# Moving two matmul stages of a recurrent layer across the sweep boundary, and the weight features ahead of the first normalisation

## What is computed

```python
xn = (x - mean) / sqrt(var + 1e-5)                       # over 1024 features
ab, AB = xis, exp(xis)
def rfs(z): return AB/32 * exp(z @ (ab*proj).T - 0.5*sum(z*z)*ab*ab)
s = rfs(xn) @ rfs(input_weights).T                       # feats @ weights.T
h = silu((xn @ w1.T)*w1s) * ((xn @ w2.T)*w2s)            # 1024 -> 4096
h = gelu((h @ h1.T)*h1s)                                 # 4096 -> 4096
h = gelu((h @ h2.T)*h2s)                                 # 4096 -> 4096
y = x + s * silu((h @ w3.T)*w3s)                         # 4096 -> 1024
```

## Time and profile before

| | us |
|---|---|
| median of three timed runs | 3020.2 |
| lowest and highest | 2763.45, 3207.62 |
| the profiled execution, device time | 2765.2 |
| its span, first to last instruction, slowest core (core 3) | 2763.6 |
| spans of the eight cores | 2758.9 to 2763.6 |
| TensorE busy in the span | 2629.6 (95%) |
| ScalarE, VectorE busy | 360.9, 251.2 |
| DMA queue of the weights, share of 16 engines' span | 86.4% |

### The profile page before, as it was taken

How to read it: one execution, slowest core, us unless ns; L and a number is a source line. 1 busy time by engine, 2 the same in 40 slices (tenths; PEclk the granted TensorE clock), 3 DMA queues, 4 the chain that set the end, 5 groups by cost and what they waited for, 6 DMA issues and landing times.

```text
span 2763.6 us, 28227 instructions; the slowest of 8 cores (2758.9 to 2763.6 us)
## 1 busy us (share of the span) xinstructions
PE 2629.6 (95%) x12054; PEld 1183.1 (43%) x12054; DVE 251.2 (9%) x382; ACT 360.9 (13%) x498; POOL 205.4 (7%) x391
## 2 busy tenths in 40 slices
PE   1699999999999999999999999999999999999995
PEld 0244444444444444444444444444444444444442
DVE  2213100000013300000013210000002200000001
ACT  0122101010121211010112200101012111010100
POOL 0100000000100000000010000000000000000000
PEclk9899999999999999999999999999999999999997
DMA  5818988888887899999997899999999899999993
GB/s 86 129 30 143 154 153 152 153 152 152 149 166 128 138 154 153 152 153 152 152 151 142 135 160 153 153 152 152 153 142 155 136 155 156 153 153 152 153 152 75
DMA packets 67115, 396.25 MB, mean 143 GB/s; under 512 B 7328, under 2 KB 11696, under 8 KB 21936
## 3 DMA queue, kind: packets, MB, share of 16 engines
q0 software_dynamic: 57408, 377.51, 86.4%
q1 hardware_dynamic: 9584, 16.92, 2.4%
HBM read 763.51 MB, written 8.39 MB: 279 GB/s over the span
## 4 chain that ended last, share of the span: by engine, by line
PE 94%; DMA 3%; DVE 1%; ACT 1%; issue 0%; POOL 0%; DVEq 0%; SPq 0%; ACTq 0%; POOLq 0%
PE pb L480 64%; PE pb L507 8%; PE pb L403 8%; PE pb L380 8%; PE pb L443 2%; PE pb L357 2%; DMA xt_sweep<-xT 1%; PE pb L329 1%; DMA wring<-w2p 1%; DMA xt_r<-xT 1%; ACT t L520 0%; PE pb L163 0%; PE pb L165 0%; DVE h_sb L417 0%; POOL xt_sweep L223 0%
## 5 line engine op out<-in xcount | busy, mean ns | idle before, releaser
L480 PE MATMUL pb<-h_sb,wring 128*128 128x512 bf16 x4096 | 884.7, 379 | 0.0
L480 PE MATMUL pb<-g_sb,wring 128*128 128x512 bf16 x4096 | 884.7, 379 | 0.0
L480 PEld LDWEIGHTS pb<-h_sb,wring 128*128 128x128 bf16 x4096 | 400.5, 98 | 484.8 <-issue 2.3
L480 PEld LDWEIGHTS pb<-g_sb,wring 128*128 128x128 bf16 x4096 | 400.8, 98 | 483.3
L507 PE MATMUL pb<-h_sb,wring 128*128 128x512 bf16 x1024 | 231.1, 389 | 18.8 <-ACT t L520 18.8
L380 PE MATMUL pb<-xn_fm,wring 128*128 128x512 bf16 x1024 | 233.2, 381 | 2.7 <-DMA wring<-w1p 2.7
L403 PE MATMUL pb<-xn_fm,wring 128*128 128x512 bf16 x1024 | 231.5, 379 | 0.6 <-DMA wring<-w2p 0.6
L527 DVE TENSOR_TENSOR s_sb<-t,s_sb 128x512 f32<-128x512 bf16 x32 | 22.1, 692 | 1970.5 <-ACT t L520 1967.7
L491 ACT ACTIVATE h_sb<-pb,h2s_c 128x512 bf16<-128x512 f32 x128 | 88.0, 687 | 796.4 <-PE pb L480 787.2
L491 ACT ACTIVATE g_sb<-pb,h1s_c 128x512 bf16<-128x512 f32 x128 | 88.0, 687 | 692.6 <-PE pb L480 683.1
L507 PEld LDWEIGHTS pb<-h_sb,wring 128*128 128x128 bf16 x1024 | 102.1, 100 | 147.2 <-issue 32.6
(11 more groups left out here) (72 smaller groups left out, 401.1 us busy)
## 6 DMA issues: line engine op xcount, KB each, us to landing
wring<-h1p POOLq DMA_DIRECT2D x128, 1024.0 KB, 10.2
wring<-h2p POOLq DMA_DIRECT2D x128, 1024.0 KB, 10.1
wring<-w1p POOLq DMA_DIRECT2D x32, 1024.0 KB, 14.3
wring<-w2p POOLq DMA_DIRECT2D x32, 1024.0 KB, 10.6
wring<-w3p POOLq DMA_DIRECT2D x32, 1024.0 KB, 10.0
xt_r<-xT SPq DMA_DIRECT2D x32, 256.0 KB, 5.0
y<-s_sb SPq DMA_DIRECT2D x32, 256.0 KB, 5.1
xt_sweep<-xT POOLq DMA_DIRECT2D x32, 128.0 KB, 11.7
```

The costliest lines, as they stand in the source:

```text
L480: ii = t.matmul(p[quad[og]][:, :], wring[:, slot, k8, og * 128:(og + 1) * 128], src_sb[:, kk * 8 + k8, :], start=(kk == 0 and k8 == 0), st ...
```

## The change

- `emit_wphase` and its VectorE squares move from between strip 1 and smm of sweep 0 to the very start: the squares ahead of the first `ln2_squares`, the matmuls between `ln2_stats(0)` and `ln2_bcast_affine(0, 0)`. They use `h_sb` 0 to 15.
- dot0 and smm become functions. In sweep 0 they run where they did. For sweep `s_ + 1`, dot0 is now written in sweep `s_` between h2 and w3, and smm behind the whole end of sweep `s_`, behind its adds, loads and stores. The next sweep then starts with strip 0 of FFN1.
- `emit_xts_loads(s_ + 1)` moves from the start of the sweep to behind the weight loads of strip 2, `ln2_squares` from behind strip 2 to behind strip 3, `ln2_stats` from behind strip 4 to behind strip 5.
- The block of set-up code (first DMAs, memsets, small vectors, `ring_load`) moves up in the file, in the same order; nothing in it is changed.

```diff
+        need(v, cast_sem["iwT"], 16)
+        sq_done = 0
+        for j in range(8):
+            sq_done = V(lambda j=j: v.tensor_mul(
+                h_sb[:, 2 * j:2 * j + 2, :].rearrange("p a b -> p (a b)"),
+                iw_c[j], iw_c[j]))
 
         ln2_squares(0, 0)
...
         ln2_stats(0)
+        emit_wphase()
         xn_ready_sweep = ln2_bcast_affine(0, 0)
 
-        for s_ in range(NS):
-            tok0 = s_ * TS
-
-            if s_ + 1 < NS:
-                emit_xts_loads(s_ + 1)
-
+        def emit_dot0(xn_rdy):
             need(t, cast_sem["projT"], 16)
...
-            feats_done = cS.n
+            return cS.n
+
+        def emit_smm(feats_done):
+            need(t, cS, feats_done)
+            need(t, cS, wstate["wt_done"])
+            for oc in range(8):
+                bk = oc % 4
+                guard_bank(bk)
+                for rc in range(8):
+                    ii = t.matmul(p[bk][:, :], Wt_sb[:, rc, oc * 128:(oc + 1) * 128],
+                                  feats[:, rc, :], start=(rc == 0), stop=(rc == 7))
+                stop = cT.inc(ii)
+                need(v, cT, stop)
+                need(v, d_y[oc], y_val.get(oc, 0))
+                ev = V(lambda oc=oc, bk=bk: v.tensor_copy(s_sb[:, oc, :], p[bk][:, :]))
+                bank_guard[bk] = (cV, ev)
+            return cT.n
...
-            ffn1_strip(0)
-            ffn1_strip(1)
-
             if s_ == 0:
...
+                feats_done = emit_dot0(xn_ready_sweep)
+                ffn1_strip(0)
+                ffn1_strip(1)
+                smm_last = emit_smm(feats_done)
+                first_strip = 2
+            else:
+                smm_last = smm_next
+                first_strip = 0
+
+            for ss in range(first_strip, 8):
                 ffn1_strip(ss)
                 if ss == 2 and s_ + 1 < NS:
+                    emit_xts_loads(s_ + 1)
+                if ss == 3 and s_ + 1 < NS:
                     ln2_squares(s_ + 1, smm_last)
-                if ss == 4 and s_ + 1 < NS:
+                if ss == 5 and s_ + 1 < NS:
                     ln2_stats(s_ + 1)
...
+            if s_ + 1 < NS:
+                feats_next = emit_dot0(xn_ready_sweep)
 
             sg_done = [0] * 8
...
                 y_val[dc] = d_y[dc].n
 
+            if s_ + 1 < NS:
+                smm_next = emit_smm(feats_next)
+
```

More of the change, by code:

```diff
@@ L145, in S @@
             return cS.inc(instr_fn())
[L147 to L206, removed]
@@ L287, in ring_load, with ln2_squares, ln2_stats @@
             return slot, d_wr[slot], d_wr[slot].n
+        xsq = feats
+        ln_state = {}
+        def ln2_squares(s_, smm_last):
+            need(v, cT, smm_last)
+            need(v, d_xts, d_xts.n)
+            for j in range(8):
+                V(lambda j=j: v.tensor_mul(xsq[:, j, :], xt_sweep[:, j, :],
+                                           xt_sweep[:, j, :]))
+            ln_state["sq"] = cV.n
+        def ln2_stats(s_):
+            need(t, cV, ln_state["sq"])
+            guard_bank(6)
+            guard_bank(7)
+            for j in range(8):
+                t.matmul(p[6][0:1, :], ones_b[:, 0:1], xt_sweep[:, j, :],
+                         start=(j == 0), stop=(j == 7))
+                ii = t.matmul(p[7][0:1, :], ones_b[:, 0:1], xsq[:, j, :],
+                              start=(j == 0), stop=(j == 7))
+            st = cT.inc(ii)
+            need(v, cT, st)
+            V(lambda: v.tensor_copy(rows[0:1, 0, :], p[6][0:1, :]))
+            ev = V(lambda: v.tensor_copy(rows[0:1, 1, :], p[7][0:1, :]))
+            bank_guard[6] = (cV, ev)
+            bank_guard[7] = (cV, ev)
+            V(lambda: v.tensor_scalar_mul(rows[0:1, 0, :], rows[0:1, 0, :], 1.0 / D))
+            V(lambda: v.tensor_scalar_mul(rows[0:1, 1, :], rows[0:1, 1, :], 1.0 / D))
+            V(lambda: v.tensor_mul(rows[0:1, 2, :], rows[0:1, 0, :], rows[0:1, 0, :]))
+            sv = V(lambda: v.tensor_sub(rows[0:1, 1, :], rows[0:1, 1, :], rows[0:1, 2, :]))
+            need(sc, cV, sv)
+            S(lambda: sc.activation(rows[0:1, 2, :], rows[0:1, 1, :], AF.Ln,
+                                    bias=c_eps[0:1, 0:1]))
+            rs = S(lambda: sc.activation(rows[0:1, 2, :], rows[0:1, 2, :], AF.Exp,
+                                         scale=c_nhalf[0:1, 0:1]))
+            need(v, cS, rs)
+            V(lambda: v.tensor_mul(rows[0:1, 3, :], rows[0:1, 0, :], rows[0:1, 2, :]))
+            rd = V(lambda: v.scalar_tensor_tensor(rows[0:1, 1, :], rows[0:1, 2, :],
+                                                  512.0 * EPS, rows[0:1, 2, :],
+                                                  op0=ALU.mult, op1=ALU.mult))
+            ln_state["rows"] = rd
@@ new lines, in ln2_bcast_affine @@
+        def ln2_bcast_affine(s_, ffn1_last):
+            need(t, cV, ln_state["rows"])
+            guard_bank(4)
+            guard_bank(5)
+            bc1 = cT.inc(t.matmul(p[4][:, :], ones_row[0:1, :], rows[0:1, 2, :],
+                                  start=True, stop=True))
+            bc2 = cT.inc(t.matmul(p[5][:, :], ones_row[0:1, :], rows[0:1, 3, :],
+                                  start=True, stop=True))
+            need(v, cT, bc2)
+            need(v, cT, ffn1_last)
+            for j in range(8):
+                V(lambda j=j: v.tensor_mul(ln_tmp[:, :], xt_sweep[:, j, :], p[4][:, :]))
+                V(lambda j=j: v.tensor_sub(xn_fm[:, j, :], ln_tmp[:, :], p[5][:, :]))
+            xr = V(lambda: v.tensor_copy(xn_fm[0:1, 8, :], rows[0:1, 1, :]))
+            bank_guard[4] = (cV, xr)
+            bank_guard[5] = (cV, xr)
+            xts_state["guard"] = xr
+            return xr
@@ L301, in emit_wphase @@
         def emit_wphase():
-            need(t, cV, wstate["sq_done"])
+            need(t, cV, sq_done)
             need(t, cast_sem["iwT"], 16)
@@ L306, in emit_wphase @@
             for j in range(8):
-                sqv = h_sb[:, 16 + 2 * j:18 + 2 * j, :].rearrange("p a b -> p (a b)")
+                sqv = h_sb[:, 2 * j:2 * j + 2, :].rearrange("p a b -> p (a b)")
                 t.matmul(p[4][0:1, :], ones_nh[:, 0:1], sqv[:, 0:512],
@@ L340, in build_nc @@
         ln2_stats(0)
+        emit_wphase()
         xn_ready_sweep = ln2_bcast_affine(0, 0)
-        for s_ in range(NS):
-            tok0 = s_ * TS
-            if s_ + 1 < NS:
-                emit_xts_loads(s_ + 1)
+        def emit_dot0(xn_rdy):
             need(t, cast_sem["projT"], 16)
             need(t, cast_sem["xisrow"], 16)
-            need(t, cV, xn_ready_sweep)
+            need(t, cV, xn_rdy)
             need(t, cV, cols_ready)
@@ L364, in build_nc @@
                 bank_guard[bk] = (cS, ev)
-            feats_done = cS.n
+            return cS.n
[14 more added lines that the diff above has]
+            return cT.n
+        smm_next = 0
+        feats_next = 0
+        for s_ in range(NS):
+            tok0 = s_ * TS
             h_by_strip = {}
@@ L412, in ffn1_strip @@
                     if s_ == 0:
-                        need(v, cT, wstate.get("so_mm", 0))
+                        need(v, cT, wstate["so_mm"])
                     for og in range(2):
```

## The result

| | us |
|---|---|
| before, median of 10 runs | 2766.4 |
| after, median of 10 runs | 2818.9 |
| ratio of after to before | 1.0193, 95% interval 1.0181 to 1.0204 |
| profiled execution after, device time and span | 2819.2, 2817.7 |

The kernel is slower by 1.9%.

What follows compares the result with a forecast made beforehand. TensorE was taken to bound the kernel: its matmuls plus the waits between them. Terms -22.2 + 58.7 + 6.3 + 8.1 + 3.6 = +54.5 on 2765.2 gave 2820 us, range 2798 to 2842.

Steps and rivals of the forecast that it cites:

- The start: Sweep 0 up to strip 2: weight features in idle time and earlier weight loads save 22.2 us, bounds 19 to 23.5.
- three cold restarts: After smm's three waits TensorE restarts at the lower clock, 2.1 us each, +6.3 us in all.
- dot0 for the Gelu: Between h2 and w3, dot0 waits for banks the Gelus free: 2.7 us three times, +8.1, plus +3.6 for the clock.
- w3's own wait: Between w3's two strips, the 4.7 us wait for banks 2 and 3 and the Silus stays.
- smm behind the adds: At three sweep ends smm's fifth group waits for a copy behind eight adds: 18.8 to 20.3 us each, +58.7.
- sweep 3's bound: Lower bound for smm's idling, from sweep 3's end without weight loads: eighth add at T + 23.9, 17.9 us.
- The stores: nothing.: At smm the eighth copy needs the eighth store, landed at T + 30, before its matmuls end: no cost.
- What was saved there? Nothing: the old place had no wait in it.: smm's old place, two strips into FFN1, had no wait, so moving it from there gains nothing.
- The moved loads, squares and statistics: x's loads, squares and statistics, moved later in the sweep, cost nothing; the statistics keep their 2.0 us wait.
- Quicker loads: Rival at smm: x loads speed up once TensorE stands still, stall 13 us, total 2800 us; 1 in 10.
- Early weight loads crowding out x: Rival at the start: five queued weight loads delay x's first slab by 17 to 34 us, 2837 to 2854; 1 in 10.
- Free boundary: Rival at the sweep boundary: no stall at smm and the start's gain stays, 2755 us; 3 in 100.

Runs made afterwards that it cites:

- The two runs on it: Changed kernel with smm and dot0 in their old places: 2745 us; kernel before with only x's sweep loads, squares and statistics moved: 2759 us.
- the free-banks run: Changed kernel with dot0 in banks 0, 1, 4, 5, 6, 7, 4, 5: 2814 us, 1.0182 of before.
- the last kernel: Kernel before with new banks for dot0, w3 and statistics, end x in `g1_sb`, adds behind their products, start loads reordered, later x loads moved: 2682 us.
- The eight-buffer run: Changed kernel with eight x buffers instead of two, in `g1_sb`, all loads issued at the end of h2: 2764 us, 1.0003 of before.
- the first run: Changed kernel with smm put back behind strip 1 of the next sweep, dot0 left between h2 and w3: 2842 us, 1.0283 of before.

## Where the prediction was right, and which of its steps failed

**The total, and the steps that failed.** 2820 against 2818.9: +54.5 forecast on the profiled execution's 2765.2, and spans 54.1 apart. The waits of smm and dot0 and the start's gain came where they were forecast and for the reasons given, but that the total fits to a microsecond is luck. The sizes of three terms failed, and their errors cancel. The start was put at -22.2 us and gave -19.2, so the sum was 3.0 too low there. smm's waits were put at 58.7 and were 55.7, so it was 3.0 too high there. The three cold restarts were put at 6.3, with one price of 2.1 us for every wait of 5 us or more, and cost 8.4 on the slowest core: a restart cost anything from 1.4 to 2.9 us over the eight cores, and one price hides that.

The sum was also made on one execution's time, at the lowest of the three timings. Read against the median then shown, 3020.2, the same 2820 would have meant a kernel 7% faster; ten timings have a median of 2766.4 and bear out the choice of 2765.2.

**The start: right in kind, 22.2 forecast, 19.2 measured.** Three of its terms were too small. iwT landed at 37.7, not at 36.3 to 37.2, so the statistics began 1.0 us late (48.39 against 47.36 before the change). The last Exp ahead of the rows' spread cost a wait of 1.07, which I had put at a fraction of that. And dot0 with its cold start took 18.55 us, not 17.70 as in the earlier trace rows. The weight features themselves, after 5.2 us of idling, took what was forecast. The two runs on it split the gain into some 14 and 5 us.

**dot0 for the Gelu: 8.1 and 3.6 forecast, 7.6 and 3.0 measured.** The step is confirmed by the free-banks run, where the wait is gone. That w3's own wait would stay, since it is for banks 2 and 3, is confirmed too (18.8 in all, before and after), and again by the last kernel, where other banks end it.

**smm behind the adds: 58.7 and 6.3 forecast, 55.7 and 8.4 measured.** Order of VectorE's stream, chain of two-buffer loads, restart at the lower clock: each as written, and taking the chain away took 38.5 of the 55.7 us. The waits were shorter mostly after sweep 2, 16.8 where 20.3 was forecast from that sweep's own adds: the eighth add ended at T + 22.9 there, not at T + 26.3. With sweep 3's bound at 17.9 the range's low end had been drawn a little too high. The restarts cost 2.7 to 2.9 each on this core and not 2.1, at the upper end of my bounds each time. Over the eight cores the means, 56.8 and 6.1, lie nearer the forecast; the time is set by one core, which had the shortest waits and the longest restarts.

**"The stores: nothing."** Right for the changed kernel. The eight-buffer run shows how near it was: without the x chain the first store holds the copies by up to 2.5 us.

**"What was saved there? Nothing: the old place had no wait in it."** True of the rows, and the weakest sentence of the text. The old place was free because dot0 stood in front of it, in two ways: 15.5 us of TensorE's time beside the adds, and 15.5 us in which no weight slot came free. The expectation of the first run has the first way; the second stands in no text of mine, and it is the larger: it turned the 9 us of waiting that I had computed into 27. For the time of the changed kernel this played no part, since the stall stands in dot0's place and keeps the ring quiet just as well, but the plain remedy of moving smm back would have made the kernel slower still.

**The moved loads, squares and statistics.** No wait for weights behind them, and none at the rows' spread in the later sweeps; the three waits of 2.0 us each stayed. Nothing was the right price.

**The rivals.** Quicker loads: a little, and not to its 13 us of stall. The medians in the three boundaries were 5.4, 4.2 and 4.7 us against 6.0, 4.8 and 6.5 before, yet the eighth add ended at T + 25.2, 25.9 and 22.9, so it was earlier in the last alone; why there is open. The 2.6 us of the fit in the Trainium skill's "DMA: Bandwidth & Descriptors", "Anatomy of one DMA — SWDGE (gpsimd) path", was not reached by any load into `xt_r` on any core (3.0 at the least); the section gives the fit for the GpSimd path, and these loads are SyncE's. Early weight loads crowding out x: no; they went out at 8.2 us and x's squares ran at 44.1, held by VectorE's work on the input weights and not by a load. Free boundary: no, each boundary had its stall. The chance of 0.48 for "within 2%" and 0.50 for slower stood on a line that the measurement, 1.0193, also nearly touches.

## What to carry to other kernels

Before a stage is moved to a point where another engine is still catching up, write down what that engine has in its queue there: a short copy behind eight adds costs what the adds cost, loads and all. Ask also what the stage that now comes early sets free, since freed slots start transfers, and these share the engines with the loads that the slow chain waits for. And where a chain of small buffered loads hides beside other work, look for a buffer that is idle just then (here `g1_sb`): eight pieces loaded ahead took the chain out of every order that was tried.

## What the runs showed of the hardware

- Loads of 256 KB into `xt_r` took 5.4 us at the median in a boundary where no weight load went out from T + 1.2 to T + 46.9, and 10.6 us beside two weight loads and a slab of x. The Trainium skill says ("DMA: Bandwidth & Descriptors", section "Queues, rings and completion order") that each DMA engine goes round between the queues that have work. By that rule a load on SyncE's queue would keep a share beside the weights' queue, and the trace agrees: it went at about half its pace.
- After 17 to 21 us of idling 32 matmuls took 8.5 to 10.0 us instead of 7.07, in all 24 cases on the eight cores; on the slowest the granted clock was 0.50 (1.2 GHz) from 809 to 817 us and 0.75 from 817 to 821, with the restart at 813.4. After 2.5 us of idling 72 matmuls took 15.70 us in 20 cases of 24 and 17.2 in four. After the 2.0 us ahead of the statistics their 16 matmuls took 5.2 us instead of 3.5 in 17 cases of 48, both kernels together. So a short wait costs its restart only sometimes, a long one each time, by an amount that varies.
- Work put into an idle time doesn't keep the next restart warm if a shorter idle time is left behind it: 5.2 us ahead of the weight features still cost 2.2 (33.43 us for 144 turns of 0.216).
